# Audio tower on one Trainium2 core: the drain of the convolution pipeline reordered, first statistics on ScalarE, four low parts on GpSimd

## Chip, core and metric

One core of a Trainium2 chip. The metric is device time in microseconds, the median of several executions.

## The reference, cut to what matters

The reference is five residual stages on a batch of 16 rows of 128x1024. The change touches the end of the first stage and the start of the second:

```python
h = conv1d(x, conv_in_w, stride=1, pad=3)                       # 64 -> 128 channels, 2048 long
h = gelu(groupnorm1(h, gn1_w, gn1_b))
h = conv1d(h, dw_w, stride=2, pad=2, groups=H) + dw_b           # five taps, 1024 long
h = conv1d(h, pw_w)
h = gelu(groupnorm1(h, gn2_w, gn2_b))                           # _L0_tok_ref
h = h + attn(_layernorm(h))                                     # _L0_attn_ref: q, k, v projections, rope, ...
...
_layernorm(x) = (x - mean(x)) / sqrt(var(x) + 1e-5)             # over the 1024 elements of a row
```

## The kernel before, in words

All of h stays in SBUF as 16 batches of 128x1024. To keep float32 accuracy each operand of a large product is split into a high part (cast to fp32r) and a low part (the rest), and a product takes three matmuls: high by high, high by low, low by high.

**conv_stage** (L224) is a software pipeline over 16 batches and 20 iterations `it`, written out by hand for each engine. In iteration `it`, TensorE runs the input convolution of batch `it` into the four banks `cv_cp`, the pointwise product of batch `it-3` (L632) into the two banks `cv_pp`, and two small products with a matrix of 1/128 (`average`, L624) that spread sums over the partitions. VectorE runs `tail(it-1)` (15 short dependent operations that make scale and shift of both group norms, L463 to L475, ended by the semaphore `coef`), `head(0, it-1)` and `head(1, it-3)` (bn_stats, L447), `taps` of batch `it-2` (L486, four of the five taps in two pairs) and `middle(it)` (L457 to L460). ScalarE splits the next input (L373), applies the Gelus (`gelu2` of batch `it-4` into h, L397; `gelu1` of batch `it-2`, L402), makes tap 0 (L405) and evacuates the convolution's banks in two halves (L379). GpSimd subtracts the low part of the next input (L351), released by `coef`. So a chain runs through each iteration: average, middle, average, tail, gelu2, pointwise, head.

**The drain.** From iteration 16 on no new batch comes in (`from_end(it)` is 4 in iteration 16, 1 in iteration 19). The first work of attention is laid between the last steps of the pipeline: the layer norm of the first quarter (batches 0 to 3), the transpositions of its rows, and the projections of the first head group, six tiles of weights of 128x1024.

- `QuarterRows`: VectorE's `stats` (L170, eight bn_stats), `coefficients` and `keep` at the end of iteration 15 give rstd and shift; ScalarE's `normalize` (L192) writes qr_xn, two buffers; TensorE's `turn` (L204) transposes a batch into two of the banks `cv_cp` (units c = 0, 1); ScalarE's `high` (L212) casts a unit into qr_xhi; VectorE's `low` (L220) subtracts into qr_xlo. Each batch after the first waits for the low part of the one before, since all use the same two banks.
- `Projections`: SP loads tile j+2 after the low part of tile j (`load`, L135; two buffers); ScalarE's `split_w` (L754) casts the high part, from tile 2 on after the projection of tile j-2; VectorE's `low_w` (L758) subtracts the low part; `project` (L801 to L803, 24 matmuls of 128x512) needs both, for tile 0 all eight low parts of the rows, for j of 2 and more the rope of an earlier tile; `rope_out` (L780 to L785) is four operations on VectorE; `v_out` and `turn_v` (L763, L810) end the block.
- TensorE's order in iterations 16 to 19 is in `last_16` to `last_19` under `pe`'s `ending`, VectorE's in the functions of the same names under its own; ScalarE's order follows the `from_end(it)` tests in its body.

Every engine takes its instructions strictly in this order, and waits on semaphores by count. After the block, attention runs with TensorE as the bound.

Of the kernel before, what the change touches and what calls it, by code (L numbers as in the profile page):

```python
# [20 lines left out]
P = 128  # L21
# [116 lines left out]
class QuarterRows:  # L138
# [6 lines left out]
    def __init__(self, nc, ctx, h, ident):  # L145
        def sb(n, shape, dt=F32):
            return ctx.enter_context(nc.sbuf_tensor(f"qr_{n}", shape, dt))

        def sem(n):
            return ctx.enter_context(nc.semaphore(f"qr_{n}"))  # L150

        self.h, self.ident = h, ident

        self.x_hi, self.x_lo = (sb(n, [P, KT, QT], F32R) for n in ("xhi", "xlo"))
        sb("line_after", [P, 24])
        self.xn = [sb(f"xn{i}", [P, L]) for i in range(2)]
        self.st, self.mv = sb("st", [P, QB, 2, 6]), sb("mv", [P, QB, 2])
        self.var, self.tmp, self.root, self.rstd, self.shift = (
            sb(n, [P, QB]) for n in ("var", "tmp", "root", "rstd", "shift"))
        self.dummy = sb("dummy", [P, 1])  # L160
        self.norm = sem("norm")
        self.normed = sem("normed")
        self.turned = sem("turned")
        self.hi_done, self.lo_done = sem("xhi_done"), sem("xlo_done")
        self.sems = [self.norm, self.normed, self.turned, self.hi_done, self.lo_done]
# [20 lines left out]

    def normalize(self, act, qt, b):

        after(act, self.norm, (qt + 1) * self.LINKS)
        if b >= 2:  # L190
            after(act, self.turned, qt * self.UNITS + 2 * b - 2)
        act.activation(self.xn[b % 2][:, :], row(self.h, qt * QB + b), ACT.Identity,  # L192
                       bias=self.shift[:, b:b + 1], scale=self.rstd[:, b:b + 1]).then_inc(self.normed, 1)

    def turn(self, pe, qt, banks, *batches):

        for b in batches:
            after(pe, self.normed, qt * QB + b + 1)
            for c in range(2):
                if b > 0:  # L200
                    after(pe, self.lo_done, qt * self.UNITS + 2 * b + c - 1)
                for k in range(KT // 2):
                    at = (c * KT // 2 + k) * P
                    last = pe.transpose(banks[:, c, k * P:(k + 1) * P], self.xn[b % 2][:, at:at + P],  # L204
                                        self.ident[:, :])
                last.then_inc(self.turned, 1)

    def high(self, act, qt, banks, b):

        for c in range(2):  # L210
            after(act, self.turned, qt * self.UNITS + 2 * b + c + 1)
            act.copy(self.x_hi[:, c * KT // 2:(c + 1) * KT // 2, b * P:(b + 1) * P],  # L212
                     banks[:, c, :].rearrange("p (k t) -> p k t", t=P)).then_inc(self.hi_done, 1)

    def low(self, dve, qt, banks, b):

        for c in range(2):
            after(dve, self.hi_done, qt * self.UNITS + 2 * b + c + 1)
            tiles, cols = slice(c * KT // 2, (c + 1) * KT // 2), slice(b * P, (b + 1) * P)
            dve.tensor_tensor(self.x_lo[:, tiles, cols], banks[:, c, :].rearrange("p (k t) -> p k t", t=P),  # L220
                              self.x_hi[:, tiles, cols].bitcast(F32), ALU.subtract).then_inc(self.lo_done, 1)


def conv_stage(nc, h, ident, ones_mean, x, conv_w, dw_w, chan, pw_wT, rope, rows, w_stage, pro):  # L224
# [8 lines left out]
    with ExitStack() as ctx:  # L233
# [65 lines left out]
        with nc.Block() as block:  # L299
# [39 lines left out]
            def _(pool):  # L339
# [22 lines left out]
                steps(pool, body)  # L362

            @block.scalar
            def _(act):
# [16 lines left out]
                def body(it, par, on):  # L382
# [4 lines left out]
                    if on(-1):  # L387
                        split_in(it + 1, 1 - par)
                    if from_end(it) == 4:
                        act.wait_ge(xlo_done, NB)  # L390
                        pro.split_w(act, 0, 0)
                        rows.high(act, 0, cp, 0)
                        rows.normalize(act, 0, 2)
                    if on(2) or on(4):
                        act.wait_ge(coef, it - 1)
                    if on(4):
                        act.activation(row(h, it - 4), pp[:, :, :], ACT.Gelu,  # L397
                                       bias=shift[:, 1:2], scale=scale[:, 1:2]).then_inc(gelu2, 1)
                    if on(2):
# [7 lines left out]
                    if from_end(it) == 4:  # L407
                        rows.high(act, 0, cp, 1)
                        rows.normalize(act, 0, 3)
                        rows.high(act, 0, cp, 2)  # L410
                        rows.high(act, 0, cp, 3)
                        pro.split_w(act, 0, 1)
                    if from_end(it) == 3:
                        pro.split_w(act, 0, 2)
                        pro.split_w(act, 0, 3)
                    if from_end(it) == 2:
                        pro.split_w(act, 0, 4)
# [4 lines left out]
                    if on(0):  # L422
                        evacuate(it, par, 0)
                        evacuate(it, par, 1)
                    if from_end(it) == 5:
                        rows.normalize(act, 0, 0)
# [4 lines left out]
            def _(dve):  # L431
# [65 lines left out]
                def body(it, par, on):  # L497
# [5 lines left out]
                    if on(1) or on(3):  # L503
                        middle(it)
                    if on(2):
                        taps(it - 2, par, (3, 4))
                    if from_end(it) == 5:
                        dve.wait_ge(gelu2, QB)
                        link = Links(dve, rows.norm, 1)
                        for b in range(QB):  # L510
                            rows.stats(dve, 0, link, b)
                        rows.coefficients(dve, link)
                        rows.keep(dve, link, rows.rstd[:, :], rows.shift[:, :])

                def ending(it, par, on):

                    def last_16():
                        tail(15)
                        heads(16, 0, on, lambda: rows.low(dve, 0, cp, 0))
                        dve.wait_ge(conv_done, NB * NCH)  # L520
                        pro.low_w(dve, 0, 0)
                        taps(14, 0, (1, 2))
                        rows.low(dve, 0, cp, 1)
                        middle(16)
                        rows.low(dve, 0, cp, 2)
                        rows.low(dve, 0, cp, 3)
                        taps(14, 0, (3, 4))
                        pro.low_w(dve, 0, 1)

                    def last_17():  # L530
# [5 lines left out]
                        pro.low_w(dve, 0, 2)  # L536
                        middle(17)
                        taps(15, 1, (3, 4))
                        pro.rope_out(dve, 0, 0, 1)
                        pro.low_w(dve, 0, 3)  # L540

                    def last_18():
                        tail(17)
                        pro.rope_out(dve, 0, 0, 2)
                        pro.low_w(dve, 0, 4)
                        heads(18, 0, on, lambda: None)
                        pro.rope_out(dve, 0, 0, 3)
                        pro.low_w(dve, 0, 5)
                        middle(18)

                    def last_19():
                        tail(18)
                        pro.rope_out(dve, 0, 0, 4)
                        pro.low_w(dve, 1, 0)
# [4 lines left out]
            def _(pe):  # L559
# [89 lines left out]
                def ending(it, par, on):  # L649

                    def last_16():
                        pe.wait_ge(raw_done, NB * 2)
                        rows.turn(pe, 0, cp, 0, 1)
                        pointwise(13, 1)
                        average(16, on, 0)
                        rows.turn(pe, 0, cp, 2)
                        average(16, on, 1)
                        rows.turn(pe, 0, cp, 3)
                        pro.project(pe, 0, 0, 0)

                    def last_17():
                        pointwise(14, 0)
                        pro.project(pe, 0, 0, 1)
                        average(17, on, 0)
                        average(17, on, 1)
                        pro.project(pe, 0, 0, 2)
# [1793 lines left out]
```

## Time and profile before

| | |
|---|---|
| median of 3 runs | 2828.05 us (2826.13 to 2829.7) |
| the profiled execution | 2826.87 us, span 2825.1 us |
| busy, share of the span | TensorE 96%, VectorE 64%, ScalarE 35%, GpSimd 4% |
| granted clock of TensorE, mean of the span | 0.985 |

A span runs from the first to the last instruction; the execution's own time lies 1.8 us above it. Times in the rows are from the start of the span. A busy TensorE is not TensorE at its peak, since matmuls are pipelined; idle time of an engine that nothing waits for costs nothing. In a timeline a row can stand for several instructions of one kind (x8), the bracket gives the idle time ahead of it and what ended that.

### The profile page before, as it was taken

The numbers are of one execution on the slowest core, as the hardware profiler recorded it, in microseconds if no ns is written. First come the engines' busy times: TensorE is split into PE (matmuls) and PEld (weight loads), VectorE is DVE, ScalarE is ACT, GpSimd is POOL, SyncE is SP. The second block draws the span as 40 slices with busy tenths as digits, with TensorE's granted clock in tenths as the row PEclk, the third lists the DMA queues.
The fourth block names the chain that finished last, engine by engine and source line by source line (L and its number), as shares of the span: only waits on it lengthen the run. The fifth ranks groups of instructions, "written<-read, shape, count | busy, mean of one in ns | idle before, by whom it ended". The sixth has DMA issues, their size and how long they took to land. (4 is left out here: it accounts for less than half of the span.)

```text
span 2825.1 us, 37124 instructions
## 1 busy us (share of the span) xinstructions
PE 2709.9 (96%) x13162; PEld 2240.3 (79%) x13162; DVE 1806.2 (64%) x3217; ACT 979.0 (35%) x2012; POOL 107.8 (4%) x65
## 2 busy tenths in 40 slices
PE   7996999999899999999999999899999988899999
PEld 5664788888788888887888888788888876688888
DVE  4888766666766666677666666776665665862221
ACT  3554333333433333334333333333333333542121
POOL 2110000000000000000000000000000000221110
PEclk9997999999999999999999999999999999999999
DMA  5320322223222222222222222222222224000000
GB/s 128 74 60 21 109 79 78 82 74 97 63 91 94 82 82 75 81 82 68 81 77 83 95 89 82 75 75 82 82 74 82 75 66 157 1 23 23 30 22 31
DMA packets 55327, 206.69 MB, mean 73 GB/s; under 512 B 6769, under 2 KB 7153, under 8 KB 53169
## 3 DMA queue, kind: packets, MB, share of 16 engines
q1 hardware_dynamic: 55216, 205.26, 23.0%
q8 instruction: 64, 1.05, 0.2%
q14 instruction: 47, 0.38, 0.0%
HBM read 196.85 MB, written 8.39 MB: 73 GB/s over the span
## 5 line engine op out<-in xcount | busy, mean ns | idle before, releaser
L801 PE MATMUL at_proj<-qr_xhi,at_whi 128*128 128x512 f32 x1536 | 617.8, 402 | 6.4 <-DVE qr_xlo L220 4.4
L803 PE MATMUL at_proj<-qr_xhi,at_wlo 128*128 128x512 f32 x1536 | 602.4, 392 | 0.0
L802 PE MATMUL at_proj<-qr_xlo,at_whi 128*128 128x512 f32 x1536 | 601.0, 391 | 0.0
L960 ACT CAST at_ohi<-at_ov 128x512 fp32r<-128x512 f32 x128 | 75.0, 586 | 847.2 <-PE at_ov L1204 847.2
L801 PEld LDWEIGHTS at_proj<-qr_xhi,at_whi 128*128 128x128 f32 x1536 | 290.4, 189 | 64.0 <-issue 4.1
L803 PEld LDWEIGHTS at_proj<-qr_xhi,at_wlo 128*128 128x128 f32 x1536 | 289.8, 189 | 63.9
L802 PEld LDWEIGHTS at_proj<-qr_xlo,at_whi 128*128 128x128 f32 x1536 | 290.8, 189 | 57.2 <-issue 0.5
L1222 PE MATMUL at_out<-at_wohi,at_ohi 128*128 128x512 f32 x1008 | 311.2, 390 | 4.0 <-DVE at_wolo L1070 3.0
L1222 PE MATMUL at_out<-at_wohi,at_olo 128*128 128x512 f32 x1008 | 310.9, 390 | 0.0
L1222 PE MATMUL at_out<-at_wolo,at_ohi 128*128 128x512 f32 x1008 | 310.7, 389 | 0.0
L1077 DVE TENSOR_TENSOR h<-h,at_out 128x1024 f32 (+1 forms) x126 | 152.8, 1213 | 210.9 <-PE at_out L1222 210.9
L1066 DVE TENSOR_TENSOR at_olo<-at_ov,at_ohi 128x512 fp32r<-128x512 f32 x128 | 88.3, 690 | 272.2 <-ACT at_ohi L960 272.2
L758 DVE TENSOR_TENSOR at_wlo<-at_wstage,at_whi 128x1024 fp32r<-128x1024 f32 x192 | 234.3, 1221 | 1.6 <-ACT at_whi L754 0.4
L1222 PEld LDWEIGHTS at_out<-at_wohi,at_ohi 128*128 128x128 f32 x1008 | 189.5, 188 | 43.7 <-issue 3.2
L1222 PEld LDWEIGHTS at_out<-at_wolo,at_ohi 128*128 128x128 f32 x1008 | 189.5, 188 | 39.5
L1222 PEld LDWEIGHTS at_out<-at_wohi,at_olo 128*128 128x128 f32 x1008 | 189.5, 188 | 39.4
L948 ACT ACTIVATE at_probs<-at_sc,at_ntop 128x128 f32<-128x128 f32 x512 | 181.0, 366 | 102.8 <-DVE at_ntop L1044 102.5
L754 ACT CAST at_whi<-at_wstage 128x1024 fp32r<-128x1024 f32 x192 | 203.1, 1058 | 18.4 <-PE at_proj L803 18.4
L1070 DVE TENSOR_TENSOR at_wolo<-at_ostage,at_wohi 128x1024 fp32r<-128x1024 f32 x128 | 153.5, 1221 | 1.5 <-ACT at_wohi L941 1.4
L941 ACT CAST at_wohi<-at_ostage 128x1024 fp32r<-128x1024 f32 x128 | 131.8, 1059 | 35.5 <-DMA at_ostage<-in_w_o_dram 35.3
L1185 PEld LDWEIGHTS at_sc<-at_k,at_q 128*128 128x128 f32 x1024 | 132.0, 192 | 11.6 <-issue 4.2
L1185 PE MATMUL at_sc<-at_k,at_q 128*128 128x128 f32 x1024 | 135.7, 276 | 3.8 <-PEq L80 3.2
(259 smaller groups left out, 3973.6 us busy)
## 6 DMA issues: line engine op xcount, KB each, us to landing
at_wstage<-in_w_qkv_dram SPq DMA_DIRECT2D x192, 512.0 KB, 3.7
at_ostage<-in_w_o_dram SPq DMA_DIRECT2D x128, 512.0 KB, 4.5
cv_x<-in_x_dram SPq DMA_DIRECT2D x32, 512.0 KB, 6.5
out_dram<-h SPq DMA_DIRECT2D x16, 512.0 KB, 2.6
fn_w_lo_raw<-in_w_t_dram SPq DMA_DIRECT2D x8, 512.0 KB, 9.8
fn_qka_lo_raw<-in_qka_t_dram SPq DMA_DIRECT2D x5, 512.0 KB, 12.0
fn_w_lo_raw<-in_dft_fwd_dram SPq DMA_DIRECT2D x4, 512.0 KB, 7.2
shared_raw<-in_a_route_dram SPq DMA_DIRECT2D x1, 544.0 KB, 4.2
```

What stands on the lines that cost most here:

```text
L754: act.copy(self.b.w_hi[j % 2][:, :], self.w_stage.buffers[j % 2][:, :]).then_inc(self.whi_done, 1)
L758: dve.tensor_tensor(self.b.w_lo[j % 2][:, :], self.w_stage.buffers[j % 2][:, :], self.b.w_hi[j % 2][:, :].bitcast(F32), ALU.subtract).then ...
L801: pe.matmul(proj[:, j % 2, :], hi[:, w], x_hi[:, k, :], start=(k == 0), stop=False)
L802: pe.matmul(proj[:, j % 2, :], hi[:, w], x_lo[:, k, :], start=False, stop=False)
L803: last = pe.matmul(proj[:, j % 2, :], lo[:, w], x_hi[:, k, :], start=False, stop=(k == KT - 1))
L941: act.copy(wo_hi[:, r, :], o_stage[r % 2][:, :]).then_inc(wohi_done, 1)
L948: last = act.activation(probs[:, r, :], sc[b % 2][:, r * P:(r + 1) * P], ACT.Exp, bias=ntop[:, r:r + 1], scale=SCALE, accum_out=total[:, r ...
L1066: dve.tensor_tensor(o_lo[:, :], ov[:, :], o_hi[:, :].bitcast(F32), ALU.subtract).then_inc(olo_done, 1)
L1070: dve.tensor_tensor(wo_lo[:, r, :], o_stage[r % 2][:, :], wo_hi[:, r, :].bitcast(F32), ALU.subtract).then_inc(wolo_done, 1)
L1077: dve.tensor_tensor(hb, hb, part, ALU.add).then_inc(added, 1)
L1185: last = pe.matmul(sc[b % 2][:, r * P:(r + 1) * P], qT[par][:, r, cols], kT[par][:, cols], start=True, stop=True)
L1222: last = pe.matmul(banks[:, c, :], a[:, rows], w[:, r, c * BANK:(c + 1) * BANK], start=first, stop=end)
```

## The change

Statistics of the first quarter move from VectorE to ScalarE: in iterations 14 and 15 ScalarE runs `sums` (two passes of Identity over a batch each, with an accumulator, and the negated mean), and, between the two halves of the evacuation, `squares` (two passes of Square about that mean). VectorE makes rstd and shift from them in `first_coefficients`, between `middle(15)` and the second pair of taps of batch 13, without bn_stats. The transpositions use all four banks, two for each of two batches (`sets=2`). GpSimd subtracts the low parts of tiles 2 to 5. The order in iterations 15 to 19 changes on ScalarE, VectorE and TensorE: on TensorE the two `average` products of iteration 16 stand behind projections 0 and 1, those of iteration 17 around projection 2.

```diff
+        self.total, self.minus, self.around = (sb(n, [P, QB]) for n in ("total", "minus", "around"))
...
+    MOMENTS = 2 * QB + QB // 2
+    def sums(self, act, *batches):
+        if batches[0]:
+            act.wait_ge(self.moments, batches[0] // 2 * 5)
+        for b in batches:
+            act.activation(self.xn[b % 2][:, :], row(self.h, b), ACT.Identity, accum_out=self.total[:, b:b + 1])\
+               .then_inc(self.moments, 1)
...
+        act.activation(self.minus[:, these], self.total[:, these], ACT.Identity, scale=-1.0 / L)\
+           .then_inc(self.moments, 1)
+    def squares(self, act, *batches):
+        act.wait_ge(self.moments, batches[0] // 2 * 5 + 3)
+        for b in batches:
+            act.activation(self.xn[b % 2][:, :], row(self.h, b), ACT.Square, bias=self.minus[:, b:b + 1],
+                           accum_out=self.around[:, b:b + 1]).then_inc(self.moments, 1)
+    def first_coefficients(self, dve):
+        link = Links(dve, self.norm, 1)
+        dve.wait_ge(self.moments, self.MOMENTS)
+        link(dve.tensor_scalar(self.var[:, :], self.around[:, :], 1.0 / L, EPS, ALU.mult, ALU.add))
+        rsqrt(dve, self.rstd[:, :], self.var[:, :], self.tmp[:, :], link)
+        dve.tensor_tensor(self.shift[:, :], self.minus[:, :], self.rstd[:, :], ALU.mult)\
+           .then_inc(self.norm, self.LINKS - link.n)
...
-                if b > 0:
-                    after(pe, self.lo_done, qt * self.UNITS + 2 * b + c - 1)
+                if b >= sets:
+                    after(pe, self.lo_done, qt * self.UNITS + 2 * (b - sets) + c + 1)
...
-                    last = pe.transpose(banks[:, c, k * P:(k + 1) * P], self.xn[b % 2][:, at:at + P],
+                    last = pe.transpose(banks[:, b % sets * 2 + c, k * P:(k + 1) * P], self.xn[b % 2][:, at:at + P],
...
             @block.gpsimd
...
+                after(pool, pro.wlo_done, 2)
+                for j in range(2, TILES):
+                    pro.low_w(pool, 0, j)
             @block.scalar
...
+                    if from_end(it) == 6:
+                        act.wait_ge(gelu2, QB)
+                        rows.sums(act, 0, 1)
+                    if from_end(it) == 5:
+                        rows.sums(act, 2, 3)
                     if from_end(it) == 4:
-                        act.wait_ge(xlo_done, NB)
-                        pro.split_w(act, 0, 0)
-                        rows.high(act, 0, cp, 0)
+                        pro.split_w(act, 0, 1)
+                        rows.high(act, 0, cp, 0, sets=2)
                         rows.normalize(act, 0, 2)
+                        rows.high(act, 0, cp, 1, sets=2)
                     if on(2) or on(4):
...
+                    if from_end(it) == 4:
+                        rows.normalize(act, 0, 3)
+                        rows.high(act, 0, cp, 2, sets=2)
+                        rows.high(act, 0, cp, 3, sets=2)
...
                     if from_end(it) == 4:
-                        rows.high(act, 0, cp, 1)
-                        rows.normalize(act, 0, 3)
-                        rows.high(act, 0, cp, 2)
-                        rows.high(act, 0, cp, 3)
-                        pro.split_w(act, 0, 1)
-                    if from_end(it) == 3:
                         pro.split_w(act, 0, 2)
                         pro.split_w(act, 0, 3)
+                    if from_end(it) == 3:
+                        pro.split_w(act, 0, 4)
                     if from_end(it) == 2:
-                        pro.split_w(act, 0, 4)
                         pro.split_w(act, 0, 5)
...
                         evacuate(it, par, 0)
+                        if from_end(it) == 6:
+                            rows.squares(act, 0, 1)
+                        if from_end(it) == 5:
+                            rows.squares(act, 2, 3)
                         evacuate(it, par, 1)
                     if from_end(it) == 5:
+                        act.wait_ge(xlo_done, NB)
+                        pro.split_w(act, 0, 0)
                         rows.normalize(act, 0, 0)
                         rows.normalize(act, 0, 1)
...
             @block.vector
...
+                    if from_end(it) == 5:
+                        rows.first_coefficients(dve)
                     if on(2):
                         taps(it - 2, par, (3, 4))
-                    if from_end(it) == 5:
-                        dve.wait_ge(gelu2, QB)
-                        link = Links(dve, rows.norm, 1)
-                        for b in range(QB):
-                            rows.stats(dve, 0, link, b)
-                        rows.coefficients(dve, link)
-                        rows.keep(dve, link, rows.rstd[:, :], rows.shift[:, :])
...
                         tail(15)
-                        heads(16, 0, on, lambda: rows.low(dve, 0, cp, 0))
+                        rows.low(dve, 0, cp, 0, sets=2)
+                        rows.low(dve, 0, cp, 1, sets=2)
                         dve.wait_ge(conv_done, NB * NCH)
                         pro.low_w(dve, 0, 0)
+                        head(1, 13, [pp[:, c, :] for c in range(2)])
+                        rows.low(dve, 0, cp, 2, sets=2)
+                        rows.low(dve, 0, cp, 3, sets=2)
+                        head(0, 15, [raw[1][:, c // 2, c % 2 * BANK:(c % 2 + 1) * BANK] for c in range(NCH)])
+                        pro.low_w(dve, 0, 1)
                         taps(14, 0, (1, 2))
-                        rows.low(dve, 0, cp, 1)
                         middle(16)
-                        rows.low(dve, 0, cp, 2)
-                        rows.low(dve, 0, cp, 3)
                         taps(14, 0, (3, 4))
-                        pro.low_w(dve, 0, 1)
...
                         taps(15, 1, (1, 2))
-                        pro.low_w(dve, 0, 2)
                         middle(17)
+                        pro.rope_out(dve, 0, 0, 1)
                         taps(15, 1, (3, 4))
-                        pro.rope_out(dve, 0, 0, 1)
-                        pro.low_w(dve, 0, 3)
...
+                        after(dve, pro.wlo_done, TILES)
                         pro.low_w(dve, 1, 0)
...
             @block.tensor
...
                         pe.wait_ge(raw_done, NB * 2)
-                        rows.turn(pe, 0, cp, 0, 1)
+                        rows.turn(pe, 0, cp, 0, 1, 2, sets=2)
                         pointwise(13, 1)
+                        rows.turn(pe, 0, cp, 3, sets=2)
+                        pro.project(pe, 0, 0, 0)
                         average(16, on, 0)
-                        rows.turn(pe, 0, cp, 2)
+                        pro.project(pe, 0, 0, 1)
                         average(16, on, 1)
-                        rows.turn(pe, 0, cp, 3)
-                        pro.project(pe, 0, 0, 0)
...
                         pointwise(14, 0)
-                        pro.project(pe, 0, 0, 1)
                         average(17, on, 0)
+                        pro.project(pe, 0, 0, 2)
                         average(17, on, 1)
-                        pro.project(pe, 0, 0, 2)
```

In `last_18` VectorE's `low_w` of tiles 4 and 5 goes too; TensorE's `last_18` and `last_19` stay.

## Rows read from the trace of the kernel before

**Rows 1.** Windows of the drain: stretch, its length, busy time per engine, granted clock, DMA.
```profile
228.50:241.60 13.10, 0.09 (x1) 0.00 (x0) 11.73 (x38) 1.91 (x3) 0.00 (x0) 0.61 0.04 11
241.60:264.00 22.40, 11.69 (x41) 8.40 (x41) 15.48 (x36) 13.79 (x16) 0.00 (x0) 0.58 0.08 24
```

**Rows 2.** Timeline of TensorE in the drain: start us, us, instruction, count, idle before.
```profile
241.68 1.94 PE L204 MATMUL cv_cp<-ident,qr_xn 128*128 128x128 f32 x8 [13.09 <-ACT qr_xn L192]
...
248.73 3.49 PE L632 MATMUL cv_pp<-cv_y,cv_pw 128*128 128x512 f32 x4
...
263.94 0.77 PE L801 MATMUL at_proj<-qr_xhi,at_whi 128*128 128x512 f32 x1 [1.49 <-DVE qr_xlo L220]
264.50 0.63 PE L802 MATMUL at_proj<-qr_xlo,at_whi 128*128 128x512 f32 x1
264.93 0.63 PE L803 MATMUL at_proj<-qr_xhi,at_wlo 128*128 128x512 f32 x1
...
271.86 1.88 PE L632 MATMUL cv_pp<-cv_y,cv_pw 128*128 128x512 f32 x4
...
281.17 0.48 PE L801 MATMUL at_proj<-qr_xhi,at_whi 128*128 128x512 f32 x1
...
293.79 1.88 PE L632 MATMUL cv_pp<-cv_y,cv_pw 128*128 128x512 f32 x4
...
302.23 0.48 PE L801 MATMUL at_proj<-qr_xhi,at_whi 128*128 128x512 f32 x1
...
307.55 0.39 PE L803 MATMUL at_proj<-qr_xhi,at_wlo 128*128 128x512 f32 x1
```

**Rows 3.** Timeline of VectorE in the drain.
```profile
228.18 2.61 DVE L486 SCALAR_TENSOR_TENSOR cv_y<-cv_g,cv_dww,cv_y 128x1024 f32<-128x1024 f32 x2
230.83 5.79 DVE L170 BATCH_NORM_STATS2 qr_st<-h 128x6 f32<-128x512 f32 x8
...
240.52 0.16 DVE L470 TENSOR_SCALAR cv_var<-cv_sp 128x2 f32<-128x2 f32 x1 [0.27 <-DVE qr_shift L183]
...
243.28 0.16 DVE L475 TENSOR_TENSOR cv_shift<-cv_ch,cv_tmp 128x2 f32<-128x2 f32 x1
...
246.16 1.29 DVE L220 TENSOR_TENSOR qr_xlo<-cv_cp,qr_xhi 128x512 fp32r<-128x512 f32 x2
...
252.26 0.70 DVE L447 BATCH_NORM_STATS2 cv_st<-cv_pp 128x6 f32<-128x512 f32 x1 [0.88 <-PE cv_pp L632]
253.00 0.20 DVE L450 BATCH_NORM_AGGREGATE cv_mv<-cv_st 128x2 f32<-128x12 f32 x1
...
272.13 0.69 DVE L780 TENSOR_TENSOR at_k<-at_proj,at_cs 128x512 f32<-128x512 f32 x1 [1.74 <-PE at_proj L803]
```

**Rows 4.** Timeline of ScalarE in iteration 15.
```profile
220.33 1.21 ACT L397 ACTIVATE h<-cv_pp,cv_shift,cv_scale 128x1024 f32<-128x1024 f32 x1 [4.71 <-DVE cv_shift L475]
...
228.09 1.01 ACT L379 COPY cv_raw<-cv_cp 128x1024 f32<-128x1024 f32 x1 [2.41 <-PE cv_cp L606]
```

**Rows 5.** Groups of instructions by line, ScalarE and GpSimd: busy us, mean ns, idle before.
```profile
L192 ACT ACTIVATE qr_xn<-h,qr_shift,qr_rstd 128x1024 f32 x8 | 9.8, 1248 | 2.6 <-DVE qr_shift L183 2.6
L948 ACT ACTIVATION_READ_ACCUMULATOR at_probs<-at_sc,at_ntop 128x1 f32 x512 | 104.3, 204 | 0.0
L2035 ACT ACTIVATE shared_raw<-ls_out 128x1024 f32<-128x1024 f32 x8 | 8.2, 1024 | 12.6 <-PE ls_out L2274 11.2 <-POOL shared L2004 1.5
L402 ACT ACT_TABLE_LOAD x1 | 1.3, 1283 | 0.0
L351 POOL TENSOR_TENSOR cv_xlo<-cv_x,cv_xhi 128x1028 fp32r<-128x1028 f32 x16 | 38.9, 2433 | 168.2 <-DVE cv_shift L475 136.4 <-ACT cv_xhi L373 22.3 <-PE cv_cp L594 9.5
```

**Rows 6.** Timeline near 2400 us, in a later stage: GpSimd and VectorE.
```profile
2399.70 2.36 POOL L1310 TENSOR_TENSOR fn_qka_lo<-fn_qka_lo_raw,fn_qka_hi 128x1024 fp32r<-128x1024 f32 x1 [18.10 <-ACT fn_qka_hi L1304]
2399.90 2.18 DVE L55 TENSOR_TENSOR shared_raw<-shared_raw 128x4 f32<-128x4 f32 x1
```

**Rows 7.** The page's DMA issues: size of each, us from issue to landing.
```profile
at_wstage<-in_w_qkv_dram SPq DMA_DIRECT2D x192, 512.0 KB, 3.7
```

More of the change, by code:

```diff
@@ L160, in __init__ @@
         self.dummy = sb("dummy", [P, 1])
+        self.total, self.minus, self.around = (sb(n, [P, QB]) for n in ("total", "minus", "around"))
+        self.moments = sem("moments")
         self.norm = sem("norm")
@@ L185, in keep @@
         assert link.n == self.LINKS
+    MOMENTS = 2 * QB + QB // 2
[5 more added lines that the diff above has]
+               .then_inc(self.moments, 1)
+        first, n = batches[0], batches[0] // 2 * 5 + 2
+        act.wait_ge(self.moments, n)
+        these = slice(first, first + 2)
+        act.activation(self.minus[:, these], self.total[:, these], ACT.Identity, scale=-1.0 / L)\
[12 more added lines that the diff above has]
+           .then_inc(self.norm, self.LINKS - link.n)
     def normalize(self, act, qt, b):
@@ L193, in normalize, with turn @@
                        bias=self.shift[:, b:b + 1], scale=self.rstd[:, b:b + 1]).then_inc(self.normed, 1)
-    def turn(self, pe, qt, banks, *batches):
+    def turn(self, pe, qt, banks, *batches, sets=1):
         for b in batches:
@@ L199, in turn, with high @@
             for c in range(2):
-                if b > 0:
-                    after(pe, self.lo_done, qt * self.UNITS + 2 * b + c - 1)
+                if b >= sets:
+                    after(pe, self.lo_done, qt * self.UNITS + 2 * (b - sets) + c + 1)
                 for k in range(KT // 2):
                     at = (c * KT // 2 + k) * P
-                    last = pe.transpose(banks[:, c, k * P:(k + 1) * P], self.xn[b % 2][:, at:at + P],
+                    last = pe.transpose(banks[:, b % sets * 2 + c, k * P:(k + 1) * P], self.xn[b % 2][:, at:at + P],
                                         self.ident[:, :])
                 last.then_inc(self.turned, 1)
-    def high(self, act, qt, banks, b):
+    def high(self, act, qt, banks, b, sets=1):
         for c in range(2):
@@ L212, in high, with low @@
             act.copy(self.x_hi[:, c * KT // 2:(c + 1) * KT // 2, b * P:(b + 1) * P],
-                     banks[:, c, :].rearrange("p (k t) -> p k t", t=P)).then_inc(self.hi_done, 1)
-    def low(self, dve, qt, banks, b):
+                     banks[:, b % sets * 2 + c, :].rearrange("p (k t) -> p k t", t=P)).then_inc(self.hi_done, 1)
+    def low(self, dve, qt, banks, b, sets=1):
         for c in range(2):
@@ L219, in low @@
             tiles, cols = slice(c * KT // 2, (c + 1) * KT // 2), slice(b * P, (b + 1) * P)
-            dve.tensor_tensor(self.x_lo[:, tiles, cols], banks[:, c, :].rearrange("p (k t) -> p k t", t=P),
-                              self.x_hi[:, tiles, cols].bitcast(F32), ALU.subtract).then_inc(self.lo_done, 1)
+            dve.tensor_tensor(self.x_lo[:, tiles, cols],
+                              banks[:, b % sets * 2 + c, :].rearrange("p (k t) -> p k t", t=P), self.x_hi[:, tiles, cols].bitcast(F32), ALU.subtract).then_inc(self.lo_done, 1)
 def conv_stage(nc, h, ident, ones_mean, x, conv_w, dw_w, chan, pw_wT, rope, rows, w_stage, pro):
@@ L544, in last_18 @@
                         pro.rope_out(dve, 0, 0, 2)
-                        pro.low_w(dve, 0, 4)
                         heads(18, 0, on, lambda: None)
                         pro.rope_out(dve, 0, 0, 3)
-                        pro.low_w(dve, 0, 5)
                         middle(18)
```

## The prediction

> **What bounds the kernel now.** Read the windows first. TensorE is the bound of almost the whole program; the exception is the drain of the convolution pipeline, where attention begins. From 228.5 to 241.6 us TensorE does nothing, from 241.6 to 264 it is busy for about half, and its granted clock is 0.61 and 0.58, mostly the lower of its levels (1.2 of 2.4 GHz) [rows 1]. Then read TensorE's own timeline for who ends each gap: 13.09 us before the first transposition of normalized rows, ended by ScalarE's qr_xn; the first projection waits for the last qr_xlo at 263.94 [rows 2]. VectorE's timeline says why: after the taps at 228.18 it takes the statistics of four batches and their coefficients, from 230.83 to the first tail link at 240.52, 9.4 us with everything queued behind them [rows 3]. ScalarE meanwhile has gaps of 4.71 us (before the Gelu of iteration 15) and 2.41 us (before its last evacuation) [rows 4]. So what decides is the path through VectorE, ScalarE and TensorE from 228 us to the last projection; once attention runs, TensorE is full, and a microsecond won in the drain is one won at the end.
>
> **The sum is made against the profiled execution**, 2826.87 us (span 2825.1); the median of the three runs, 2828.05, lies 1.18 above it, and I carry the difference over. I give times "before" from rows, "after" from stepping the new order through the same durations. Batches and tiles are numbered as in the code.
>
> **1. Statistics.** Sums: two passes of about 1.25 us (an Identity over 128x1024 takes 1.248 [rows 5]), each with an accumulator read of 0.20 that mostly overlaps [rows 5], and one tiny scaling: some 2.9 us in ScalarE's gap of 4.71, so nothing; the iteration before repeats the pattern. If the cover went, the Gelu that frees the pp banks would be late and the convolution with it. Squares: no row shows Square with an accumulator over 1024 columns; Square itself runs at 1.024 from PSUM [rows 5]. Bounds: 2x1.05 and 2x1.6 us; I take 2x1.3, nearest the Identity row. From 225.7 (2.41 before 228.09 [rows 4]) they end at 228.3, just when VectorE has finished middle(15); the last evacuation loses 0.2 at most. VectorE's 9.4 us become 13 links. The tail's 15 links run from 240.52 to 243.44 [rows 3], 0.195 each, so 13 are 2.55: coefficients from 228.4 to 230.95, then taps 3 and 4 (2.64), then tail(15) from 233.6 to 236.5. Before it ended at 243.44: **6.9 earlier**. The new wait holds taps(13) and all behind it in VectorE's queue; at 2x1.6 it would cost 0.6.
>
> **2. To the first projection.** Normalized rows come from 231 on; two sets of banks let batches 0 and 1 be transposed without VectorE. Batch 2 waits for the first low part (237.2) and runs to 239.1. Pointwise(13) waits for gelu2(12), which ScalarE ends at 238.6 after tail(15), and starts at 239.1. At the low clock its second half reaches VectorE 3.53 us later (248.73, 252.26 [rows 2, 3]): statistics end at 243.35, aggregation 243.55 (0.20), four low parts (two in 1.29 [rows 3]) 246.2. Project(0) starts at 246.35 instead of 263.94 [rows 2]: **17.6 earlier**. head(0,15), low_w(0,1) and taps(14), which stood ahead, now run beside project(0).
>
> **3. Given back.** Average(16) now stands behind project(0) and project(1), so tail(16) no longer runs beside the projections but after two of them. Project(0) takes 7.92 as before (263.94 to 271.86 [rows 2]; it begins at the low clock). Project(1) takes 5.7, as project(5) does at the full clock (302.23 to 307.94 [rows 2]). With 0.3 for each average, 2.85 for tail(16) and 1.3 for gelu2(13), pointwise(14) would follow project(0)'s start by 18.4; before, 7.92.
>
> Now GpSimd. The subtractions of tiles 2 to 5 leave VectorE and take GpSimd 2.4 each (the same kind took 2.433 [rows 5]). Tile 3's high part is cast when project(1) ends; GpSimd starts 1.15 us after that end, in the middle of tail(16). The trace has this meeting elsewhere: a GpSimd subtraction from 2399.70 to 2402.06, and VectorE's 128x4 product, begun at 2399.90, took 2.18 instead of 0.16 [rows 6]. A tail is made of such operations from SBUF alone. So tail(16) loses 2.4, tile 4 meets tail(17) in the same way (2.3), tile 2 meets taps(14), where VectorE would wait for average(16) anyhow, and tile 5 meets operations with an operand in PSUM. Bounds for one meeting: 0 and 2.4; I take the whole.
>
> So pointwise(14) follows project(0) by 20.8: **12.85 back, net 4.75 earlier**. Pointwise(14) to project(2): before 9.31 (271.86 to 281.17 [rows 2]), with project(1) between. After: 3.53 for pointwise at the low clock (TensorE has waited 7 us), 0.70 and 0.20 for statistics [rows 3], 0.35 for the average: 4.8. **4.5 gained, net 9.25.** Project(2) to pointwise(15): before 12.6. After, VectorE's chain: two taps 2.64, middle 0.66, a rope 2.78 (four of the 0.69 kind [rows 3]), two taps 2.64, less the 0.35 already passed, then tail(17) 2.85, its meeting 2.3, gelu2(14) 1.3: 14.8. **2.2 back, net 7.05.** Project(3) ends about a microsecond before that, so this chain bounds, barely. Pointwise(15) to project(5) and its end: 8.4 and 5.7 as before [rows 2]; up to 2.2 more if project(4) starts at the low clock as project(0) does (7.92 less 5.7); the gap ahead of it is short, so I take 0.
>
> **Edits at nothing.** Tile 1 is split earlier, in ScalarE's wait for transpositions. SP's loads keep their rule (tile j+2 after low part j) and land 3.7 us later [rows 7]; GpSimd's late low parts still free the buffers over 10 us ahead of use. The new wait in last_19 (all six low parts) holds only low_w(1,0); GpSimd is done long before. Nothing is queued behind GpSimd's waits. Should tile 4's load come late, project(4) would wait for it.
>
> **Sum:** 7.0 us: 2819.9 by the profile, **2821.0** for the median.
>
> **A rule beside it.** Of meetings of VectorE with GpSimd the 2.18 row already told. The Trainium skill ("SBUF — State Buffer", SBUF: two separate sides) says that the loser "fully blocks", and that VectorE instructions with two SBUF inputs count when GpSimd reads SBUF; the trace agrees, 2.18 against 0.16. It speaks against this change: without it the sum would be 11.4 instead of 7.0.
>
> **Rivals.**
> (a) The meetings cost nothing, because casts or tails fall elsewhere. Then tail(16) gives 2.4 and tail(17) 2.0 (the rest under project(3)): gain 11.4, 2816.6. Against it: both are fixed by the same end of a projection. Chance 0.25.
> (b) The gain is mostly eaten by ScalarE: Square needs another function table than Gelu, two loads in each of iterations 14 and 15. One load is 1.283 us [rows 5]. The first two hide in the gap of 4.71 and behind an evacuation; the third delays the coefficients and the fourth gelu2(12), 2.6 on the path: gain 4.4, 2823.6. Against: L2035 uses Square and has no load of its own [rows 5]. With passes of 1.6 us and project(4) at the low clock the same class is reached (7.0 less 0.6 and 2.2: 4.2). Chance 0.18. The Trainium skill ("ScalarE: Activation LUTs", Table sets) lists relu, copy, identity and abs as in every set and does not name Square; at its 2.66 us a switch this case would lose about 5 and gain 2.
> (c) **Slower.** The shorter pieces leave TensorE at 1.2 GHz all through the drain: gaps of 4 to 7 us before transpositions and pointwise products, in a stretch that now has 0.58. A projection at that level is 24x0.427 = 10.2 (264.50 to 264.93 is one step [rows 2]) against 5.7. Extra: project(0) 2.3, project(1) 4.5, project(2) beyond VectorE's chain 2.2, project(3) 3.7, project(4) and (5) 4.5 each: 21.7, less 7.0: 14.7 slower, 2842.7. It decides from two whole projections on (9.0 over 7.0). Against: before, project(0) came back to the full clock in its own course. Chance 0.05.
> That the change does nothing is excluded: 9.4 us of statistics leave the only engine that all wait for.
>
> **Numbers.** A difference of 0.2%, 5.65 us, is about what a measurement here can tell from none. Forecast 0.52, about three quarters of it over 5.65 (0.39), the rest below (0.13). Faster: 0.39+0.25 = 0.64; same 0.13+0.18 = 0.31; slower 0.05. The range takes in (a) with some spread, to 2815, and the bounds of (b), to 2826.
>
> **What would show it.** Right: no bn_stats on h in the drain; project(0) near 246 us; GpSimd's second and third subtraction inside tail(16) and tail(17), with one link of 2 us each; pointwise(14) after a TensorE gap of some 7 us; project(5) near 295. Wrong: a table load by the squares; tails of 2.9 us beside GpSimd; projections at 0.63 us a matmul throughout; an idle TensorE before 228.

## The result and the profile after

The changed kernel takes 2845.45 us (median of 4 runs, 2841.59 to 2846.85) where the kernel before takes 2827.09 beside it: a ratio of 1.0065, interval 1.0052 to 1.0077, so 18.4 us **slower**. Forecast was 2821.0, a gain of 7. The profiled execution took 2846.64 us, its span is 2844.8, and the granted clock of the whole span is 0.985, the same as before.

Where the time went is read from two views of windows, cut at TensorE's first scores of attention (312.5 us before, 302.2 after) and at the same count of TensorE instructions behind them. The kernel before, its stretch and length, then the busy time per engine, the granted clock and the DMA share:

```profile
312.50:2340.00 2027.50, 1995.79 (x9594) 1670.77 (x9594) 1360.70 (x2023) 701.09 (x1683) 0.00 (x0) 0.99 0.25 81
2340.00:2826.00 486.00, 454.12 (x2486) 389.20 (x2484) 205.91 (x562) 139.26 (x210) 67.77 (x36) 0.98 0.11 42
```

The changed kernel, the same view; its first two rows answer to [rows 1]:

```profile
228.50:241.60 13.10, 8.11 (x36) 6.00 (x36) 11.41 (x34) 11.03 (x15) 0.00 (x0) 0.74 0.12 42
241.60:264.00 22.40, 13.71 (x55) 10.45 (x56) 20.74 (x38) 8.71 (x8) 5.76 (x2) 0.90 0.22 72
...
302.20:2360.00 2057.80, 2027.75 (x9594) 1677.93 (x9594) 1361.86 (x2023) 701.05 (x1683) 0.00 (x0) 0.99 0.24 80
2360.00:2845.00 485.00, 454.57 (x2486) 390.58 (x2484) 205.22 (x562) 139.35 (x210) 68.08 (x36) 0.98 0.11 42
```

The drain did what was hoped: TensorE is busy for 8.11 of 13.10 us where it did nothing, the clock there is 0.74 and 0.90 instead of 0.61 and 0.58, and the scores start 10.3 us earlier. (1.0 us of this is no part of the change: the profiled execution of before ran that much late from its start, its Gelu of iteration 4 at 67.75 us against 66.77 after, and 66.81 in the kernel of e2, which has the old order.) But attention itself, the same 9594 matmuls at the same clock, takes 2057.8 instead of 2027.5 us: **30.3 more**. The last stage is the same within 1 us.

What in it became slower is told by the view of one line: minimum, median and maximum of its matmuls in ns; then come the row of its weight loads in the groups by line and two rows of the timeline, ten starts apart. (A projection's matmul loads a 128x128 tile of the weights, its stationary operand, and then runs 512 columns of the rows, its moving operand, against it.) Of the kernel before:

```profile
L802 PE MATMUL at_proj<-qr_xlo,at_whi x1536: 387/389/628, 264.5 to 2309.3; 128*128 128x512 f32 x192
L1222 PE MATMUL at_out<-at_wohi,at_ohi x1008: 389/389/764, 335.0 to 2352.5; 128*128 128x512 f32 x168
...
L802 PEld LDWEIGHTS at_proj<-qr_xlo,at_whi 128*128 128x128 f32 x1536 | 290.8, 189 | 57.2 <-issue 0.5
...
999.80 0.39 PE L802 MATMUL at_proj<-qr_xlo,at_whi 128*128 128x512 f32 x1
...
1002.08 0.39 PE L803 MATMUL at_proj<-qr_xhi,at_wlo 128*128 128x512 f32 x1
```

And of the changed kernel, where the same line is L841:

```profile
L841 PE MATMUL at_proj<-qr_xlo,at_whi x1536: 388/397/628, 244.2 to 2328.5; 128*128 128x512 f32 x192
L1261 PE MATMUL at_out<-at_wohi,at_ohi x1008: 387/389/632, 323.9 to 2372.6; 128*128 128x512 f32 x168
...
L841 PEld LDWEIGHTS at_proj<-qr_xlo,at_whi 128*128 128x128 f32 x1536 | 291.2, 190 | 64.0 <-issue 0.5
...
999.66 0.39 PE L841 MATMUL at_proj<-qr_xlo,at_whi 128*128 128x512 f32 x1
...
1002.00 0.40 PE L842 MATMUL at_proj<-qr_xhi,at_wlo 128*128 128x512 f32 x1
```

The projection's matmuls have a median of 397 ns where it was 389; those of the output projection (at_out), of the same shape, stayed at 389. A weight load takes as long as before (189 and 190); only the idle time between loads grew. The ten starts take 2.34 us (999.66 to 1002.00), 0.234 each; before, they took 2.28 (999.80 to 1002.08), 0.228 each. The difference, 0.006 by these rounded times, is 28 us on the 4608 projection matmuls, near the 30.3. The diff does not touch these matmuls. What it does touch is the memory in front of their weights: `self.total, self.minus, self.around` are allocated at the end of QuarterRows, ahead of all tensors of attention. Bytes from the start of a partition in the two compiled programs:

```
                 before     after
qr_xhi            83200     83200     moving rows
at_whi0          132864    132960     stationary weights, high part
at_wlo1          145152    145248     stationary weights, low part
```

Before, all are multiples of 256; after, the weights lie 96 bytes on, and the rows do not. (The kernel already has an unused tensor of 24 floats, 96 bytes, called line_after, behind the moving rows.)

TensorE in the drain of the changed kernel, the rows that answer to [rows 2]:

```profile
231.21 3.01 PE L237 MATMUL cv_cp<-ident,qr_xn 128*128 128x128 f32 x16 [3.62 <-ACT qr_xn L225]
...
243.87 0.47 PE L840 MATMUL at_proj<-qr_xhi,at_whi 128*128 128x512 f32 x1 [2.77 <-DVE qr_xlo L253]
...
249.70 0.48 PE L840 MATMUL at_proj<-qr_xhi,at_whi 128*128 128x512 f32 x1
...
262.11 3.75 PE L672 MATMUL cv_pp<-cv_y,cv_pw 128*128 128x512 f32 x4 [6.42 <-ACT h L438]
...
267.14 0.47 PE L840 MATMUL at_proj<-qr_xhi,at_whi 128*128 128x512 f32 x1
...
282.04 2.49 PE L672 MATMUL cv_pp<-cv_y,cv_pw 128*128 128x512 f32 x4 [3.01 <-ACT h L438]
...
284.75 0.63 PE L841 MATMUL at_proj<-qr_xlo,at_whi 128*128 128x512 f32 x1
...
292.26 0.47 PE L840 MATMUL at_proj<-qr_xhi,at_whi 128*128 128x512 f32 x1
...
302.23 1.04 PE L1224 MATMUL at_sc<-at_k,at_q 128*128 128x128 f32 x7 [2.72 <-PEq L80]
```

VectorE, answering to [rows 3]; the last three long rows are its meetings with GpSimd:

```profile
227.18 0.17 DVE L215 TENSOR_SCALAR qr_var<-qr_around 128x4 f32<-128x4 f32 x1
...
229.63 0.16 DVE L217 TENSOR_TENSOR qr_shift<-qr_minus,qr_rstd 128x4 f32<-128x4 f32 x1
229.71 2.60 DVE L532 SCALAR_TENSOR_TENSOR cv_y<-cv_g,cv_dww,cv_y 128x1024 f32<-128x1024 f32 x2
...
235.09 0.16 DVE L521 TENSOR_TENSOR cv_shift<-cv_ch,cv_tmp 128x2 f32<-128x2 f32 x1
...
250.87 4.62 DVE L532 SCALAR_TENSOR_TENSOR cv_y<-cv_g,cv_dww,cv_y 128x1024 f32<-128x1024 f32 x2
...
256.97 2.19 DVE L55 TENSOR_TENSOR cv_tmp<-cv_rstd 128x2 f32<-128x2 f32 x1
...
272.94 4.76 DVE L532 SCALAR_TENSOR_TENSOR cv_y<-cv_g,cv_dww,cv_y 128x1024 f32<-128x1024 f32 x2
```

ScalarE in iteration 15, answering to [rows 4], and GpSimd's subtractions:

```profile
219.33 1.21 ACT L438 ACTIVATE h<-cv_pp,cv_shift,cv_scale 128x1024 f32<-128x1024 f32 x1 [2.38 <-DVE cv_shift L521]
...
225.73 1.14 ACT L208 ACTIVATE qr_xn<-h,qr_minus 128x1024 f32<-128x1024 f32 x1
226.78 0.19 ACT L208 ACTIVATION_READ_ACCUMULATOR qr_xn<-h,qr_minus 128x1 f32 x1
227.10 1.01 ACT L415 COPY cv_raw<-cv_cp 128x1024 f32<-128x1024 f32 x1
...
256.78 2.36 POOL L797 TENSOR_TENSOR at_wlo<-at_wstage,at_whi 128x1024 fp32r<-128x1024 f32 x1 [2.37 <-ACT at_whi L793]
274.23 2.40 POOL L797 TENSOR_TENSOR at_wlo<-at_wstage,at_whi 128x1024 fp32r<-128x1024 f32 x1 [15.08 <-ACT at_whi L793]
```

### The profile page after: what moved, and what is told of

Same layout as the page of the kernel before. It is cut to its first block and busy times, and to the rows that moved or that the text cites. A ratio compares the mean times of both kernels' runs of the same rounds, so it can differ in the third digit from the quotient of the medians.

```text
span 2844.8 us, 37126 instructions
## 1 busy us (share of the span) xinstructions
PE 2738.6 (96%) x13162; PEld 2244.9 (79%) x13162; DVE 1801.5 (63%) x3196; ACT 987.9 (35%) x2030; POOL 119.0 (4%) x69
## 5 line engine op out<-in xcount | busy, mean ns | idle before, releaser
L840 PE MATMUL at_proj<-qr_xhi,at_whi 128*128 128x512 f32 x1536 | 624.7, 407 | 7.3 <-DVE qr_xlo L253 5.7
L841 PE MATMUL at_proj<-qr_xlo,at_whi 128*128 128x512 f32 x1536 | 611.2, 398 | 0.0
L842 PE MATMUL at_proj<-qr_xhi,at_wlo 128*128 128x512 f32 x1536 | 610.8, 398 | 0.0
L841 PEld LDWEIGHTS at_proj<-qr_xlo,at_whi 128*128 128x128 f32 x1536 | 291.2, 190 | 64.0 <-issue 0.5
L819 DVE TENSOR_TENSOR at_q<-at_proj,at_cs 128x512 f32<-128x512 f32 x128 | 88.0, 687 | 84.5 <-PE at_proj L842 83.5
## 6 DMA issues: line engine op xcount, KB each, us to landing
fn_qka_lo_raw<-in_qka_t_dram SPq DMA_DIRECT2D x5, 512.0 KB, 12.9
```

Of the source, the lines that this page charges most:

```text
L840: pe.matmul(proj[:, j % 2, :], hi[:, w], x_hi[:, k, :], start=(k == 0), stop=False)
L841: pe.matmul(proj[:, j % 2, :], hi[:, w], x_lo[:, k, :], start=False, stop=False)
L842: last = pe.matmul(proj[:, j % 2, :], lo[:, w], x_hi[:, k, :], start=False, stop=(k == KT - 1))
```

## Experiments

Theory A: the three small tensors displace the weights of attention against the moving rows, and that costs the 30 us. Its main rival: the new order, or GpSimd's part, slows attention by itself.

### The place put back, and displaced in the old kernel (e1 to e4)

e1 and e3 add to the changed kernel, behind the three tensors, `sb("pad", [P, 40])` (e1) or `[P, 8]` (e3), so that all of attention lies 256 or 128 bytes on. e2 and e4 are the kernel before with 24 floats more: behind the last small tensor of QuarterRows, so that the weights move and the moving rows do not (e2), or ahead of the moving rows, so that both move (e4).

```diff
 # e1: changed kernel, QuarterRows
         self.total, self.minus, self.around = (sb(n, [P, QB]) for n in ("total", "minus", "around"))
+        sb("pad", [P, 40])
 # e2: kernel before, QuarterRows
         self.dummy = sb("dummy", [P, 1])
+        sb("pad", [P, 24])
 # e4: kernel before, QuarterRows
+        sb("pad", [P, 24])
         self.x_hi, self.x_lo = (sb(n, [P, KT, QT], F32R) for n in ("xhi", "xlo"))
```

> The changed kernel plus one unused tensor of 160 bytes a partition behind the three new ones, so that all tensors allocated after them lie 256 bytes further than in the kernel before, not 96. Nothing computed changes. Theory A (the time is lost because the weight tiles lie 96 bytes off): the projections' matmuls go back from a median of 397 to 389 ns, attention from 2057.8 to about 2027.5 us, and the 10 us won in the drain stay: about 2817 us. Theory B (the new order itself slows attention, whatever the addresses): 397 ns and about 2845 us as before.

> The kernel before plus one unused tensor of 96 bytes a partition at the place where the changed kernel has its three new ones; nothing else changes. Theory A (place of the weights): projections at 397 ns instead of 389, about 2857 us (2827 + 30). Theory B (the new order): 389 ns and 2827 us.

> The changed kernel with an unused tensor of 32 bytes a partition behind the new ones, a shift of 128 bytes in all. If the place of the weights counts and lines of 128 bytes or less matter: 389 ns and about 2817 us, as with a shift of 256. If only multiples of 256 do: 397 ns and about 2845 us. Theory B (the order): 397 ns and 2845 us too, and then e1 as well.

> The kernel before plus an unused tensor of 96 bytes a partition ahead of qr_xhi, so that the moving rows (qr_xhi, qr_xlo) and the weights lie 96 bytes further together. If what counts is where the weights lie by themselves: 397 ns and about 2857 us. If it is where they lie relative to the moving rows: 389 ns and about 2827 us.

**Measured.** e1: 2819.36 us (8 runs, 2814.56 to 2822.12; before 2827.76, 11 runs), ratio 0.9971, interval 0.9961 to 0.9982. One run each of the others: e2 2851.66, e3 2841.15, e4 2830.54. The view of the same line, for e1:

```profile
L842 PE MATMUL at_proj<-qr_xlo,at_whi x1536: 387/389/628, 244.7 to 2297.1; 128*128 128x512 f32 x192
```

e2:

```profile
L803 PE MATMUL at_proj<-qr_xlo,at_whi x1536: 388/397/628, 262.8 to 2334.1; 128*128 128x512 f32 x192
```

e3:

```profile
L842 PE MATMUL at_proj<-qr_xlo,at_whi x1536: 387/393/632, 245.1 to 2323.1; 128*128 128x512 f32 x192
```

e4:

```profile
L803 PE MATMUL at_proj<-qr_xlo,at_whi x1536: 387/389/628, 263.4 to 2311.4; 128*128 128x512 f32 x192
```

**What follows.** 160 bytes of padding turn the changed kernel from 18.4 us slower into 8.4 us faster, and 96 bytes make the old kernel 24 us slower (e2, one run against 2827.76; 30 were expected) with nothing else changed: the order is innocent. It is the place of the weights against the rows that counts, since moving both by 96 costs nothing that one run can tell (e4: 389 ns). 128 bytes off is still slow: e3's 393 ns lie between the 389 and the 397 that were expected. 256 off is not slow (e1).

### Which tensors count (e5, e9, e10)

e5 leaves all displaced tensors of the changed kernel 96 bytes off, but puts the four split-weight tensors back on multiples of 256. e9 is the mirror: e1 with those four alone 96 bytes off. e10 is e5 again, with more runs.

```diff
 # e5 and e10: changed kernel; e9: e1, with 24 floats ahead and 40 behind
+        sb("pad_ahead", [P, 40])
         self.w_hi = [sb(f"whi{i}", [P, L], F32R) for i in range(2)]
         self.w_lo = [sb(f"wlo{i}", [P, L], F32R) for i in range(2)]
+        sb("pad_behind", [P, 24])
```

> The changed kernel with 160 unused bytes a partition just ahead of the four buffers of split weights (at_whi, at_wlo) and 96 just behind them: these four lie 256 bytes from their old place, everything else of attention (staging, q, k, probabilities, output weights) stays off the old multiple. Theory A1 (the place of the split weights relative to the moving rows decides alone): projections at 389 ns, about 2817 us. Theory A2 (the staging buffers or other tensors of attention matter, through the casts or the loads): 397 ns and about 2845 us, or something between.

> The changed kernel with 160 bytes behind its three small tensors (as in e1, 2819.4 us), and then with the four split-weight tensors alone moved on by 96 bytes: everything else lies where e1 has it. Theory A1 (only the place of the split weights against the moving rows counts): all 4608 projection matmuls take 397 ns again (start to start 0.235 us instead of 0.228), some 30 us: 2847 to 2852. Theory A2 (the weights are about two thirds of it and other displaced tensors the rest, as e5's one run of 2825.1 suggested): 20 to 26 us more than e1, 2839 to 2846, with the projection at 395 to 397 ns and the matmuls of the output projection (at_out) at 389. Rival (the weights' place is innocent and e5 gained by something else that its pads moved): 2817 to 2823, projection at 389 ns.

> The kernel of e5 again, timed against the kernel before: the changed kernel with only the four split-weight tensors back at multiples of 256 bytes, all other displaced tensors left 96 bytes off. Theory A1 (only the weights count): as e1, 2817 to 2822, a ratio near 0.997. Theory A2 (the other displaced tensors cost 5 to 10 us by themselves): 2823 to 2830, a ratio of 0.999 to 1.001, with the output projection's matmuls at 391 to 392 ns as in e5's one look. Rival (e5's single run was a chance low one): 2835 or more.

**Measured.** e5: 2825.12 (one run). For the other two the kernel before took 2825.64 beside them (13 runs). e9: 2846.53 (4 runs, 2845.38 to 2848.43), ratio 1.0070, interval 1.0053 to 1.0086. e10: 2824.15 (10 runs, 2822.26 to 2829.75), ratio 0.9999, interval 0.9989 to 1.0008. A row of at_out in the groups by line (busy us, mean ns of one) of e1, where all tensors are in place:

```profile
L1262 PE MATMUL at_out<-at_wohi,at_ohi 128*128 128x512 f32 x1008 | 311.3, 390 | 4.0 <-DVE at_wolo L1110 3.0 <-DVE at_olo L1106 1.0
```

The line's view and that row of e9:

```profile
L844 PE MATMUL at_proj<-qr_xlo,at_whi x1536: 392/397/632, 244.6 to 2328.4; 128*128 128x512 f32 x192
...
L1264 PE MATMUL at_out<-at_wohi,at_ohi 128*128 128x512 f32 x1008 | 313.5, 392 | 4.0 <-DVE at_wolo L1112 3.0 <-DVE at_olo L1108 1.0
```

and of e10:

```profile
L843 PE MATMUL at_proj<-qr_xlo,at_whi x1536: 387/389/628, 243.7 to 2304.0; 128*128 128x512 f32 x192
...
L1263 PE MATMUL at_out<-at_wohi,at_ohi 128*128 128x512 f32 x1008 | 314.5, 393 | 4.0 <-DVE at_wolo L1111 3.0 <-DVE at_olo L1107 1.0
```

**What follows.** Displacing the four weight tensors alone is enough for the whole loss: e9 lies 27.2 above e1 and level with the changed kernel (A1, though 0.5 us under its range, and with at_out a little slower too). Putting them alone back recovers 21.3 of the 26.1 us between the changed kernel and e1 (A2). The two do not add: with the weights in place, 4.8 us by the times (7.9 by the ratios to the kernel before beside each) still hang on the other displaced tensors. The groups by line say where most of that is lost: the three rows of at_out sum to 939.7 us in e10 against 932.9 in e1, while those of the projection are back (1815.6 against 1817.5). But at_out's own operands do not explain it by their place alone. In the changed kernel they lie 96 off as in e10, and its three rows sum to 934.1; in e9 they are in place, and the rows sum to 937.0. Which tensor's place counts there stays open; no run moved them one by one.

### What each part of the change is worth (e6 to e8)

All three have the padding of e1. e6 gives the four subtractions back to VectorE, e7 leaves them on GpSimd but holds two of them until VectorE's tail is over, and e8 is the kernel before with the statistics of the change alone, in the old order.

```diff
 # e6: e1, plus low_w(dve, 0, j) behind taps(14) (j=2) and behind ropes 0, 2, 3 (j=3, 4, 5)
-                after(pool, pro.wlo_done, 2)
-                for j in range(2, TILES):
-                    pro.low_w(pool, 0, j)
...
-                        after(dve, pro.wlo_done, TILES)
 # e7: e1
                 for j in range(2, TILES):
+                    if j in (3, 4):
+                        pool.wait_ge(coef, NB + j - 3)
                     pro.low_w(pool, 0, j)
 # e8: kernel before, plus the three tensors, the pad, sums(), squares() and first_coefficients()
-                        for b in range(QB):
-                            rows.stats(dve, 0, link, b)
-                        rows.coefficients(dve, link)
...
+                        rows.first_coefficients(dve)
```

> e1 with the low parts of tiles 2 to 5 back on VectorE (tile 2 behind the taps of batch 14, tile 3 behind the first rope, tiles 4 and 5 behind the third and fourth). Theory C (the meetings with GpSimd cost what the waiting tail lost in e1, 2.3 us in tail(16) and 2.3 in tail(17), on the path): pointwise(14) 2 us earlier, the scores start at 297 to 299 us instead of 301.1, the time 2 to 4 us below e1. Theory D (taking the four subtractions off VectorE was worth it): four times 1.2 us come back on VectorE's path, the scores start at 302 to 306 and the time is 1 to 5 us above e1.

> e1 with GpSimd's subtractions of tiles 3 and 4 held until tail(16) and tail(17) have ended (a wait on the semaphore that a tail ends with, as the kernel does for its input split). Theory C: both tails take 2.9 us again, the scores start at about 297 us, the time is 3 to 4.5 us below e1, some 0.9955 of the kernel before. Rival: the held subtractions meet the next operations instead (the ropes' last additions) and project(4) waits for tile 4: no gain over e1.

> The kernel before with only the statistics on ScalarE (sums, squares, first_coefficients), with 160 unused bytes so that the weights lie 256 bytes off; drain order, two banks and low parts on VectorE as before. Theory E (the statistics alone are worth the 6.9 us by which tail(15) ends earlier, and the rest of the drain follows): the scores start at about 305.7 us instead of 312.6, the time is about 2821 us, ratio 0.9976. Theory F (the gain needs the new order too, since the old one has the transpositions wait for VectorE anyway): less than 3 us.

**Measured**, beside 2826.83 for the kernel before (15 runs). e6: 2814.22 (5 runs, 2811.92 to 2816.48), ratio 0.9958, interval 0.9944 to 0.9972. e7: 2813.96 (5 runs, 2813.33 to 2818.08), 0.9962, 0.9948 to 0.9976. e8: 2819.59 (11 runs, 2817.99 to 2822.28), 0.9977, 0.9968 to 0.9986. TensorE's timeline of e1, the wait for tail(16), the one for tail(17), and the scores:

```profile
262.67 3.75 PE L673 MATMUL cv_pp<-cv_y,cv_pw 128*128 128x512 f32 x4 [6.79 <-ACT h L439]
...
282.56 1.95 PE L673 MATMUL cv_pp<-cv_y,cv_pw 128*128 128x512 f32 x4 [1.89 <-ACT h L439]
...
301.06 1.69 PE L1225 MATMUL at_sc<-at_k,at_q 128*128 128x128 f32 x8 [2.88 <-PEq L80]
```

VectorE's of e1, one link in each of the two tails:

```profile
257.00 2.33 DVE L56 SCALAR_TENSOR_TENSOR cv_tmp<-cv_tmp,cv_var 128x2 f32<-128x2 f32 x1
...
276.33 2.29 DVE L52 TENSOR_SCALAR cv_tmp<-cv_var 128x2 int32<-128x2 int32 x1
```

TensorE's of e6:

```profile
259.87 3.63 PE L673 MATMUL cv_pp<-cv_y,cv_pw 128*128 128x512 f32 x4 [4.34 <-ACT h L436]
...
277.52 1.96 PE L673 MATMUL cv_pp<-cv_y,cv_pw 128*128 128x512 f32 x4 [1.02 <-ACT h L436]
...
297.25 1.97 PE L1225 MATMUL at_sc<-at_k,at_q 128*128 128x128 f32 x8 [3.19 <-PEq L80]
```

and of e8:

```profile
238.92 1.94 PE L238 MATMUL cv_cp<-ident,qr_xn 128*128 128x128 f32 x8 [6.54 <-DVE qr_xlo L254]
...
255.19 0.77 PE L839 MATMUL at_proj<-qr_xhi,at_whi 128*128 128x512 f32 x1 [1.49 <-DVE qr_xlo L254]
...
302.81 0.37 PE L1223 MATMUL at_sc<-at_k,at_q 128*128 128x128 f32 x1 [3.14 <-PEq L80]
```

**What follows.** Without the meetings the scores come 3.8 us earlier than in e1 (297.25 against 301.06; 297.10 in e7), the sum of what the two waits lost, 2.45 and 0.87, and a little more; the intervals of e1 and e6 overlap by a little, so the profile carries this, not the times alone. That e7 is as good as e6 shows that the time at which GpSimd works costs, not that it works; but also that freeing VectorE of four subtractions of 1.22 us gains nothing measurable. The statistics alone give 7.2 us (e8, the time of theory E, though its scores come 2.9 us earlier than E had them, 1.0 of it the late start of before); the new order adds 5.4 to that where no meeting eats it (e6 against e8, timed together, their runs apart). In the change as it is, order and GpSimd cancel to about a microsecond (e1, 8.4). **The best kernels here are e6 and e7**, 12.6 and 12.9 us under the kernel before by the medians.

## Why the prediction was wrong

**The step that failed** is the premise under the sum, "once attention runs, TensorE is full, and a microsecond won in the drain is one won at the end", together with "Edits at nothing", in which the three small tensors do not appear at all. They had a price of some 27 us (e9 against e1, 27.2; the changed kernel against e1, 26.1), through the place of the weights. None of the rivals covers it: (c) has the sign and nearly the size (2842.7) but another cause, a low clock in the drain, and the drain's clock rose.

The terms of the sum came near in total, some of them by cancelling:
- **Statistics** (6.9 earlier): tail(15) ends at 235.25 instead of 243.44, 8.2 earlier, of which 1.0 is the late start of before. The squares took 1.15 and 1.14, not 2x1.3, and their reads 0.19. No table load stands in front of them (ScalarE's loads before and behind them start at 39.21 and 302.00), so rival (b) falls.
- **To the first projection** (17.6 earlier): 243.87 for 263.94, 20.1, or 19.1 without the start.
- **Given back**: pointwise(14) follows project(0) by 18.2 us instead of the 20.8 I worked out, since project(0) ran at the full clock from its start (5.83 us to 249.70; I took 7.92). The meeting inside tail(16) came as worked out: one link of 2.19 us at 256.97. Pointwise(14) to project(2): 5.0 (4.8 worked out). Project(2) to pointwise(15): 14.9 (14.8), but by other means: tile 4's subtraction at 274.23 met the taps (4.76 us for two instead of 2.60), not tail(17); in e1 it met tail(17). Pointwise(15) to project(5): 10.2 instead of 8.4, the start of project(4) at the low clock (0.63 us a matmul until 286.5), for which I took 0 of a bound of 2.2.
- **The sum**: in the changed kernel the drain by itself won 9.0 (project(5) at 292.26 for 302.23, less the 1.0 of the start) instead of 7.0: 1.5 more at the first projection and 2.6 less given back behind it, against 1.8 more lost at project(4). In the time, 8.4 was measured in e1, with the place put right. That this lies so near to 7.0 is partly luck, since the misses had both signs. Rival (a), no meetings, was given 11.4: e6 and e7 measured 12.6 and 12.9.

The clue was there before. In the trace of before, the convolution's matmuls have the same shape as the projection's and another time. View of one line, from 60 to 220 us, where the clock is full:

```profile
L585 PE MATMUL cv_cp<-cv_xlo,cv_whi x71: 387/397/400, 63.6 to 219.9; 128*128 128x512 f32 x71
```

397 ns against 389, with the unused tensor line_after in the source: one instruction, one shape, two prices, and I did not ask why. That the convolution's 397 ns have the same cause was not tried.

## What to carry to other kernels

A new tensor, however small, moves all that is allocated behind it: list it in the diff as an edit with a price, and compare the addresses of the big operands of the bound engine before and after. Where instructions of one kind and shape show two durations in the trace at one clock, find out why before costing anything at nothing. And when a kernel becomes slower with fewer waits, compare the median of its commonest instruction first: 6 ns from start to start on 4608 matmuls outweighed all that the drain gained.

## What was unexpected of the hardware

- The fp32r matmul of 128x512 took 389 ns in the median, 0.228 us from start to start, with its stationary tile and its moving rows both on multiples of 256 bytes, 397 (0.234) with the weights 96 bytes off, 393 to 395 with 128 off, and 389 again with both 96 off (one run each of the last two). The weight loads' own time stayed at 188 to 190 ns. Why is not shown by any of these runs, nor what other distances cost.
- Meetings of VectorE with GpSimd hold for the smallest operations: links of 128x2 took 2.19, 2.33 and 2.29 us instead of 0.16, and a pair of 1024-column taps 4.62 and 4.76 instead of 2.60. The 128x4 row [rows 6] was a good price for all of them.
